# Routing nine of sixteen batches through a 103-tile expert stage, and a new instruction order in a merged attention

## What is computed

```python
x = x + tanh(g_xattn[0]) * L0_xattn(ln(x), ...)   # long convolution ("hyena")
x = x + tanh(g_ffn[0])   * L0_ffn(ln(x), gate_w, w_gate, w_up, w_down)
x = x + tanh(g_xattn[1]) * L1_xattn(...);  x = x + tanh(g_ffn[1]) * L1_ffn(...)
x = x + tanh(g_xattn[2]) * L2_xattn(...);  x = x + tanh(g_ffn[2]) * L2_ffn(...)
x = x + tanh(g_xattn[3]) * L3_xattn(...);  x = x + tanh(g_ffn[3]) * L3_ffn(...)
```

```python
probs = softmax(x @ gate_w); w, sel = top_k(probs, 8); w = w / sum(w)
pos = rank of each (token, choice) within its expert, in token order
keep = pos < 1024
y = (silu(x @ w_gate[e]) * (x @ w_up[e])) @ w_down[e]
out[token] = sum over kept choices of w * y
```

## Time and profile before

| what | value |
|---|---|
| median of 3 runs | 2677.8 us (2677.27 to 2686.52) |
| profiled execution | 2674.28 us, of which the recorded span is 2672.4 |
| PE busy | 2308.8 us, 86% of the span |
| DVE, ACT, POOL busy | 1410.1 (53%), 1123.0 (42%), 654.3 (24%) |
| hyB, where the weight loads are issued | starts at 41 us, DMA share 0.42 until 129 |
| gate0 | 143 to 190 us |
| moe | 191 to 733 us |
| l1x, l1f | 733 to 1236 us |
| l2x | 1236 to about 2103 us; one batch in its middle: 51.5 us (1600.08 to 1651.61) |
| l3x, l3f | 2103 to 2672 us; l3f from 2403, its tiles from 2513 to 2577 |

### The profile page before, as it was taken

The page is one execution under the profiler, slowest core; times in us unless marked ns, Lnnn a source line. Parts: engine busy times, 40 slices in busy tenths (PEclk is TensorE's granted clock), DMA queues, the critical chain, the costliest instruction groups (busy, mean ns, idle before and its releaser), DMA issues. The chain is left out here.

```text
span 2672.4 us, 37871 instructions
## 1 busy us (share of the span) xinstructions
PE 2308.8 (86%) x10712; PEld 1446.3 (54%) x10760; DVE 1410.1 (53%) x3456; ACT 1123.0 (42%) x3406; POOL 654.3 (24%) x894
## 2 busy tenths in 40 slices
PE   6959999999968858885899888988989477869999
PEld 3446767666645534442555555555556244436775
DVE  7951111111145547774567677667667557764233
ACT  2022222222135525553555555655555167763332
POOL 5612222222113320001333333333333100002222
PEclk9959999999989989998999999999999689989999
DMA  6100000000030000000000000000000000022342
GB/s 250 53 7 7 7 6 6 6 6 6 2 140 1 0 3 1 0 0 24 1 1 1 1 0 0 0 0 0 0 0 0 2 5 4 4 97 101 103 126 63
DMA packets 40680, 68.91 MB, mean 26 GB/s; under 512 B 6800, under 2 KB 34448, under 8 KB 39312
## 3 DMA queue, kind: packets, MB, share of 16 engines
q1 hardware_dynamic: 37520, 59.44, 6.5%
q0 software_dynamic: 3072, 8.39, 1.0%
HBM read 51.30 MB, written 16.52 MB: 25 GB/s over the span
## 5 line engine op out<-in xcount | busy, mean ns | idle before, releaser
L820 DVE TENSOR_TENSOR moe_hid<-moe_act_g,moe_pU 128x384 f32<-128x384 f32 x128 | 70.9, 554 | 443.4 <-ACT moe_act_g L792 443.4
L792 ACT ACTIVATE moe_act_g<-moe_pG 128x384 f32<-128x384 f32 x128 | 62.7, 490 | 424.5 <-PE moe_pU L747 424.5
L726 POOL TENSOR_TENSOR moe_hidw<-moe_hid,moe_data_w_all 128x384 f32<-128x384 f32 x128 | 105.7, 826 | 426.7 <-DVE moe_hid L820 419.9
L979 PE MATMUL l2x_pQ<-big,l2x_xT 128*128 128x512 f32 x320 | 161.5, 629 | 39.8 <-POOL l2x_cT L2227 32.8
L2080 ACT ACTIVATE l2x_prob<-l2x_pS,l2x_nb,l2x_rms_q 128x256 f32<-128x256 f32 x256 | 142.5, 565 | 120.0 <-DVE l2x_nb L2306 120.0
L747 PE MATMUL moe_pG<-big,moe_xT 128*128 128x384 f32 x512 | 187.5, 489 | 4.1 <-POOL moe_xT L714 4.1
L768 PE MATMUL moe_pO<-big,moe_hT 128*128 128x256 f32 x768 | 186.8, 379 | 0.0
L747 PE MATMUL moe_pU<-big,moe_xT 128*128 128x384 f32 x512 | 186.3, 486 | 0.0
L2061 ACT ACTIVATE l2x_square<-l2x_pQ 128x128 bf16<-128x128 f32 x384 | 101.4, 292 | 102.2 <-PE l2x_pQ L979 102.2
L768 PEld LDWEIGHTS moe_pO<-big,moe_hT 128*128 128x128 f32 x768 | 136.0, 190 | 13.2
L747 PEld LDWEIGHTS moe_pU<-big,moe_xT 128*128 128x128 f32 x512 | 97.6, 191 | 68.3 <-issue 0.9
(11 more groups left out here) (453 smaller groups left out, 5248.7 us busy)
## 6 DMA issues: line engine op xcount, KB each, us to landing
route_x<-l3f_zero SPq DMA_DIRECT2D x1, 4992.0 KB, 16.3
l3f_xg<-route_x SPq DMA_DIRECT2D x39, 128.0 KB, 2.2
route_y<-l3f_y SPq DMA_DIRECT2D x39, 128.0 KB, 1.7
big<-in_f_gu SPq DMA_DIRECT2D x1, 4096.0 KB, 12.5
big<-in_e_gate SPq DMA_DIRECT2D x1, 3072.0 KB, 10.4
big<-in_e_up SPq DMA_DIRECT2D x1, 3072.0 KB, 17.3
big<-in_e_down SPq DMA_DIRECT2D x1, 3072.0 KB, 24.2
moe_lanes<-in_l2f_lanes SPq DMA_DIRECT2D x16, 192.0 KB, 2.8
```

The source lines that it names most:

```text
L726: pool.tensor_tensor(hidw[c % 2][:].rearrange("p (e i) -> p e i", e=n), hid[c % 2][:].rearrange("p (e i) -> p e i", e=n), bc(w, chunk // n ...
L979: last = pe.matmul(out, lhsT=xT[:, k, :], rhs=w[:, k, cols], start=(k == 0), stop=(k == KC - 1))
```

## The change

Nine batches (0 to 8) of L0_ffn are no longer computed densely. Each of their tokens goes to the 8 tiles of its 8 experts; there are (9*128*8 + 32*127)//128 = 103 tiles. Order: batches 9 to 12 dense (32 items), 103 routed tiles, batches 13 to 15 dense (24 items). The gate stage keeps the normalised tokens of batches 0 to 8 and the turned ones of 9 to 15, takes the 8 best right from the scores as each batch comes, ranks with 25 matmuls and computes the places (`slot`). The weighting of dense items moves from POOL to DVE, since POOL now scatters (72 indirect DMAs, paced by `gu_ps`, the count of finished ups) and gathers (72). The gate and up weights are laid side by side per expert (`e_gu`), and the down weights are loaded a second time with the 96 hidden rows of an expert on partitions 0 to 95 (`e_downx`), into `small`, whose own load therefore comes after the last tile. The table is cleared by one DMA from a zero input in HBM, behind the weights in hyB, and both routed stages use it.

```diff
-                G["load"](sp, "moe")
-                G["load"](sp, "small")
+                G["load"](sp, "gate")
+                G["load"](sp, "moe")
+                G["load"](sp, "zero")
...
+            if what == "zero":
+                sp.dma_start(G["route_x"].rearrange("(j p) c -> p j c", p=P),
+                             D["c_zero"].unsqueeze(1).to_broadcast([P, L0["NT"], C])).then_inc(sems["zero"], 16)
```

The gate stage, DVE and PE:

```diff
+            def best(b):
+                dve.wait_ge(logits, b + 1)
+                ch(dve.max(top[:, b, :], logit(b)))
+                ch(dve.match_replace(replaced[:, b, :], top[:, b, :], logit(b), FLOOR))
...
+            dve.tensor_scalar(chosen[:], replaced[:], FLOOR, None, ALU.is_equal).then_inc(masks, 1)
...
+            ch(dve.tensor_tensor(prod[:], need[:].unsqueeze(1).to_broadcast([P, NE, NE]),
+                                 below[:].rearrange("p (e f) -> p e f", e=NE), ALU.mult))
+            ch(dve.tensor_reduce(offs[:], prod[:], AX.X, ALU.add))
...
+            pe.wait_ge(const_in, 48)
+            pe.wait_ge(masks, 1)
+            picked = chosen[:].rearrange("p b e -> p (b e)")
+            pe.matmul(pR[:], lhsT=lower[:], rhs=picked, start=True, stop=True)
+            for d in range(1, B):
+                pe.matmul(pR[:, d * NE:], lhsT=onesb[:], rhs=picked[:, 0:(B - d) * NE], start=False, stop=True,
+                          skip_group_check=True)
+            for b in range(SB):
+                last = pe.matmul(pC[:, 0:NE], lhsT=onesb[:], rhs=chosen[:, b, :], start=(b == 0), stop=(b == SB - 1))
```

The new expert stage `phase_l0_ffn`:

```diff
+        @block.sync
+            sp.wait_ge(scattered, 16 * TOPK * SB)
+            for j in range(XR):
+                load(j)
...
+            for j in range(NT):
+                if j + 4 + XR < NT:
+                    sp.wait_ge(turned, at["routed", j + 4] + 1)
+                    load(j + 4 + XR)
+                sp.wait_ge(out_read, outs["routed", j] + 1)
+                sp.dma_start(dy[j * P:(j + 1) * P, :], y[j % YR][:]).then_inc(y_out[j % YR], 16)
...
+            sp.wait_ge(down_done, R1)
+            sp.wait_ge(combined, 1)
+            G["load"](sp, "small")
+            for n in range(lanes_early + 3, B):
+                lanes.load(sp, n)
+        @block.gpsimd
+            for b in range(SB):
+                for k in range(TOPK):
+                    pool.wait_ge(gu_ps, 1 + 5 * (TOPK * b + k) // 12)
+                    pool.indirect_dma_start(dx, bass.IndirectOffsetOnAxis(slot_i[:, b, k:k + 1], 0), G["xn_kept"][b][:],
+                                            None).then_inc(scattered, 16)
+            for r in range(YR):
+                pool.wait_ge(y_out[r], 16 * len(range(r, NT, YR)))
+            for b in range(SB):
+                if b >= GR:
+                    pool.wait_ge(combined, b - GR + 1)
+                for k in range(TOPK):
+                    pool.indirect_dma_start(yk[b % GR][:, k, :], None, dy,
+                                            bass.IndirectOffsetOnAxis(slot_i[:, b, k:k + 1], 0)
+                                            ).then_inc(yk_in[b % GR], 16)
...
+        @block.tensor
+                    pe.wait_ge(turn_read, at["routed", i] + 1)
+                    for k in range(KC):
+                        last = pe.matmul(pG[q % 2][:, 0:2 * HID], lhsT=xgT[i % 2][:, k, :],
+                                         rhs=W["e_gu"][:, k, bass.ds(expert[i] * 2 * HID, 2 * HID)], start=(k == 0),
+                                         stop=(k == KC - 1))
...
+            for q in range(Q + 2):
+                if q < Q:
+                    up(q)
+                if R0 <= q + 2 < R1:
+                    turn_routed(q + 2 - R0)
+                if 0 < q <= Q:
+                    turn_hidden(q - 1)
+                if q >= 2:
+                    down(q - 2)
...
+        @block.vector
+            def own():
+                dve.wait_ge(const_in, 16)
+                ch(dve.tensor_tensor(passed, bc(starts[:], NE),
+                                     G["until"][0:1, :].unsqueeze(1).to_broadcast([1, NT, NE]), ALU.is_ge))
+                ch(dve.tensor_reduce(owner[:], passed, AX.X, ALU.add))
+                    dve.tensor_tensor(hid[q % 2][:], act_g[q % 2][:], pU[q % 2][:, 0:CH], ALU.mult).then_inc(gated, 1)
+                    dve.wait_ge(gated, n + 1)
+                    dve.tensor_tensor(hidw[q % 2][:].rearrange("p (e i) -> p e i", i=HID),
+                                      hid[q % 2][:].rearrange("p (e i) -> p e i", i=HID),
+                                      bc(w_all[:, i, c * EC:(c + 1) * EC], HID), ALU.mult).then_inc(ready, 1)
+            def combine(b):
+                dve.wait_ge(yk_in[b % GR], 16 * TOPK * (b // GR + 1))
+                for k in range(TOPK):
+                    ch(dve.scalar_tensor_tensor(x, yk[b % GR][:, k, :], weight[:, b, k:k + 1], x, ALU.mult, ALU.add))
```

The merged attention, the slot lists of PE, ACT and POOL:

```diff
-                if at_least(b, g, 1):
-                    turn_probs(*before(b, p, g, 1), 1)
                 if at_least(b, g, 2):
                     output(*before(b, p, g, 2))
+                if at_least(b, g, 1):
+                    turn_probs(*before(b, p, g, 1), 1)
                 if g >= 2 and not last:
                     trans(b + 1, 1 - p, g - 2)
-                if at_least(b, g, 1):
-                    values(*before(b, p, g, 1), 2 * b + (1 if g == 0 else 2))
                 f_second(b, g)
                 if g < 2:
                     trans(b, p, g + 3)
+                if at_least(b, g, 1):
+                    values(*before(b, p, g, 1), 2 * b + (1 if g == 0 else 2))
                 if g == 0:
                     value_rows(b, p, 0)
...
                 exps(b, g, 1)
-                if at_least(b, g, 1):
-                    probs(*before(b, p, g, 1), 1)
-                f_middle(b, g)
                 if g == 2:
                     evacuate(b, p, 5)
                 if g < 2:
                     squares(b, p, g + 4)
                 elif not last:
                     squares(b + 1, 1 - p, 1 if g == 2 else 3)
+                if at_least(b, g, 1):
+                    probs(*before(b, p, g, 1), 1)
+                f_middle(b, g)
                 if g >= 2 and not last:
                     evacuate(b + 1, 1 - p, g - 2)
+                if g < 2:
+                    evacuate(b, p, g + 3)
                 if at_least(b, g, 1):
                     values(*before(b, p, g, 1))
-                if g < 2:
-                    evacuate(b, p, g + 3)
...
+                if g == 0 and not last:
+                    ctx(b + 1, 1 - p)
                 f_middle(b, p, g)
                 if not last:
                     if g == 1:
-                        ctx(b + 1, 1 - p)
                         unit(b + 1, 1 - p, 0)
```

The last stage: ten early batches instead of eight, batches 8 to 15 turned in one group, the routing steps some items earlier, the table's clearing removed, scatters paced from item 10 on, gathers let off by item, and the combine of batch b at R1 + 4 + 3*b//2 instead of R1 + 4 + 2*b:

```diff
-    EARLY = B // 2
+    EARLY, PACE0 = 10, 10
...
+                    pool.wait_ge(gu_ps, PACE0 + 2 * (TOPK * b + k) // 3)
...
+                pool.wait_ge(gu_ps, min(R1 + 1 + 3 * b // 2, Q))
...
-                return R1 + 4 + 2 * b
+                return R1 + 4 + 3 * b // 2
```

More of the change, by code:

```diff
@@ new lines, in scores @@
+            def scores(b):
+                pe.wait_ge(xT_ready, b + 1)
+                if b >= 2:
+                    pe.wait_ge(steps, 2 * (b - 1))
+                for k in range(KC):
+                    last = pe.matmul(logit(b), lhsT=turned(b)[:, k, :], rhs=G["l0_gate_w"][:, k, :],
+                                     start=(k == 0), stop=(k == KC - 1))
+                last.then_inc(logits, 1)
+            pe.wait_ge(*G["loaded"]["gate"])
+            turn(0)
+            for b in range(1, B):
+                turn(b)
+                scores(b - 1)
@@ L882, in _ @@
+            last.then_inc(ranks, 1)
         @block.scalar
         def _(act):
-            front_scalar(act)
-            act.wait_ge(steps, 2)
+            for b in range(B):
+                act.wait_ge(xT_ps, b + 1)
+                if 4 <= b < SB:
+                    act.wait_ge(logits, b - 3)
+                act.activation(turned(b), pT[b % 2][:, 0:C].rearrange("p (k t) -> p k t", k=KC),
+                               ACT.Copy).then_inc(xT_ready, 1)
+            act.wait_ge(steps, 2 * B + 2)
@@ new lines, in _ @@
+            nm.statistics(dve, 0)
+            nm.statistics(dve, 1)
+            for b in range(B):
+                if b % nm.GROUP == 1 and b // nm.GROUP + 2 < B // nm.GROUP:
+                    nm.statistics(dve, b // nm.GROUP + 2)
+                if b >= SB + len(nm.ring):
+                    dve.wait_ge(xT_ps, b - len(nm.ring) + 1)
+                nm.normalise(dve, b)
+                if b >= 3:
+                    best(b - 3)
+            for b in range(B - 3, B):
+                best(b)
@@ new lines, in _ @@
+            dve.tensor_scalar(chosen[:], replaced[:], FLOOR, None, ALU.is_equal).then_inc(masks, 1)
+            for t in range(2):
+                L = pL[t][:, 0:B // 2 * NE].rearrange("p (b e) -> p b e", e=NE)
```

(8 more changed lines are left out.)

542 lines of the change are left out of this document (306 added, 236 removed).

## The result

| what | before | after |
|---|---|---|
| median, same chip | 2682.1 us (2677.3 to 2686.5, 4 runs) | 2560.1 us (2560.05 to 2561.84, 4 runs) |
| ratio | | 0.9551, 95% interval 0.9535 to 0.9567 |
| profiled execution | 2674.28 us, span 2672.4 | 2560.05 us, span 2558.0 |
| granted TensorE clock over the span | 0.949 | 0.942 |

A forecast was written before the change was run, and what follows sets the result against it. TensorE columns bound the first expert stage; merged attention left TensorE idle 90 us. Terms -157.8 (dense to routed), -8.2 (gate), +7.4 (waits), -5 (attention), +1.3 (last stage) took 2674.3 to 2512.0; plus 3, 2515 us, range 2500 to 2530.

The forecast's parts named there:

- The gate stage's tail: Gate stage after the last score: new tail shorter, experts start at 182.9 instead of 191.18, -8.2 us.
- R4: Rival: slow HBM-to-HBM clearing of the slot table holds up the gate stage's constants, total 2754 us; chance 0.02.
- The attention's mechanism: Merged attention: context-copy wait goes, new waits for quantised hidden (1.9) and row values (0.9); -5 us in the stage.
- R3: Rival: merged attention gains all 63.6 us of its named waits, less some rest, total 2465 us; chance 0.07.
- I take 1.404, since two shapes obey one column price: First expert stage: each new routed tile costs its 1664 columns, 1.404 us; 103 tiles add 144.6 us.
- R1: Rival: register load or SP's DMAs, not columns, set the tile at about 1.62 us, total 2537; chance 0.13.
- (e): Late expert stage: SP issues small weights after the first combine, lanes 13 to 15 behind them, +0.5 us.
- (c): Late dense items: batch 1's gathers come late and hold DVE, +1; gathers slowed inside combine steps, +1 us more.
- (d): End of the expert stage: the ninth batch's combine stands in front of the last finish, +1 us.
- R2: Rival: gathers, each 0.5 us longer beside DVE, set the late dense items, total 2545 us; chance 0.10.
- (a): Early expert stage: DVE's tile-owner operations at item 1 delay item 2's multiplies, +1.7 us.
- The last stage ... meet no wait: Last stage: ten early batches, pacing and removed clearing cost nothing; only combines and late gathers at the end add 1.3 us.

The follow-up runs named there:

- e8: Changed kernel with TensorE's and ScalarE's attention lists as before, only POOL's context copy one slot earlier; 2544.7 us, ratio 0.9396.
- e2: Changed kernel with tile weights sliced by constants (expert i mod 32), the register load and its check kept but unused; 2551.4 us, tiles 1.411 us.
- e3: Changed kernel without SP's 97 loads of tiles 6 to 102, stores kept; 2575.4 us, tiles 1.629 us.
- e6: Changed kernel without the bounds check on the expert's number loaded into the TensorE register; 2551.3 us, tiles 1.411 us.
- e9: Changed kernel without the first expert stage's 72 gathers and their combines, small weights issued right after the last tile; 2537.2 us.
- e12: Changed kernel with the edits of e6 and e8, and small weights issued only after seven batches are combined; 2499.8 us, ratio 0.9327.
- e14: Changed kernel with the edits of e6 and e8, and the last stage's routing steps at their old places; 2521.2 us, ratio 0.9318.
- e5: Changed kernel, unedited, run again on another chip; 2572.8 us, ratio 0.951.
- e10: Changed kernel with the whole merged attention as before, lists and context copy; 2568.1 us, ratio 0.9579.

## Why the prediction was wrong

**Right.** The gate stage's tail, -8.2 against -8.1. Dense items at 4.20. The first tile's turn, 2.2 against 2.05. The clearing, costed at nothing and put at 124: issued at 44.2 it landed 79.6 us later, at 123.8, and nobody waited (R4 falls). The last stage's tiles. The attention's mechanism: new waits of 1.7 for the hidden (1.9 forecast) and of up to 0.8 for the row values (0.9), a batch of 51.1. R3 falls for this order; with the old lists and only the copy moved (e8) the stage is 42.5 us shorter than before, where the forecast had 5 and R3 55.

**Wrong, first: "I take 1.404, since two shapes obey one column price".** The tile of the earlier trace rows sat where two limits nearly meet: 1920 columns need 1.62 us, and the same kinds of register instruction need 1.636 in the new tile. It could not tell me which binds, and I read it as proof for columns. What fails is the overlap: I let the columns hide all register work, and 1664 columns do not. R1 had the size right, 1.62 and +22, and half of the cause: load and check alone (e2) leave 1.411, SP's DMAs (e3) have no part, and it takes the slices' arithmetic on top. Measured is 1.636 over 94 tiles, 94 x (1.636 - 1.404) = +21.8, and e6 takes it away. It deserved the larger chance: the only row with the same registers showed 1.62.

**Second: (e), +0.5 for the small weights.** I priced only what SP issues late, not what 4.2 MB of weights (the 22 sizes in the DMA view sum to that, not to the 4.9 of the expectations) do to batch 1's gathers and to the lane behind them. With (c) and (d) I had 3.5 us; the waits were 1.24 + 7.14 + 2.98 + 0.23 = 11.6. e9 ties them to gathers, combines and the weights' place together; e12 puts 7.3 of 11.7 down to the weights. R2's cause, DVE steps that hold gathers back, is not it: 72 gathers took 70.2 us, 0.975 each, beside nine combines at 0.486 a step. The Trainium skill's exclusive lock ("SBUF — State Buffer", Who interferes with whom) costs little here: of the three gathers that start inside batch 0's combine (515.65, 516.89, 518.14) two took 0.94 and 0.95 us and one 1.07, and over all 72 the mean is 0.03 above 0.945, not the 0.5 of R2. (a) was 3.20 for 1.7.

**Third: "The last stage ... meet no wait".** True of tiles and clearing, not of the moved routing steps, which I put at nothing without a reason: +6.6 by e14.

**Fourth: scatter and the clock.** Two parts of the chain came out longer with no line of them changed: +4.8 in L1's stages, +6.0 in L3's attention. The rows of L3's attention show a lower clock, same stretch, before and after:

```profile
2185.00:2235.00 50.00, 41.45 (x293) 25.08 (x292) 40.05 (x100) 37.65 (x103) 3.52 (x9) 0.97 0.02 6
```

```profile
2057.00:2107.00 50.00, 41.81 (x257) 24.93 (x257) 35.14 (x88) 33.07 (x90) 2.83 (x9) 0.85 0.02 5
```

But nothing ties this to the change. The same code took 487.9 to 489.0 us in nine of the sixteen later traces of L1's stages and 492.2 to 493.5 in seven (before 488.3, after 493.0), and 291.7 to 301.3 in L3's attention (before 295.2, after 301.1). These 10.8 us lie within the scatter of single executions; why the clock differs between them was not tried.

In the experts' stretch 37.0 us were missing. Tiles are 21.8 of them and waits 8.8: 16.8 measured, less the 7.4 forecast and the 0.6 that the kernel before had in this stretch (one wait of 0.63 us). The other 6.4 are nearly all clock: the first two items took 7.6 us up to their first transposes, where before they took 6.8, and behind three of the waits the first six downs took 2.4 to 2.6 us instead of 1.3.

The attention gave 7.9 us more than forecast. Twelve full batches at 51.06 us instead of 51.53 are 5.7 of the 12.9; another 5.6 come from five batches that ran at clock 0.97 before and took 52.1 to 53.2 us. The changed kernel has none such, and neither have e5 and e8; e10, with the old lists and copy, has seven of twelve again. The sum: +21.8 + 8.8 + 6.4 + 1.2 + 4.8 - 7.9 + 6.0 + 6.8 = +47.9, from -162.3 to -114.4.

## What to carry to other kernels

- A row that satisfies two limits at once proves neither. Before an operation is made smaller, ask what else each instance of it needs (register loads, bounds checks, address arithmetic), and take the time of the like operation as its floor until an edit shows otherwise. Here dropping a bounds check on a value that was clamped already gave 21 us over 94 tiles.
- A moved load is priced by what is in flight beside it at the new place, not by its issue: here gathers landed in 6.9 us beside it and in 2.8 without. And in an in-order list, moving one late item (the context copy) gave 28 us more than moving it with the list around it.
- Before a stage's difference in one trace is explained, look how far the same code scatters in the others: 4 to 10 us here.

## What I had not expected of the hardware

- TensorE reports itself busy 99% of a stretch that its register instructions slow down by 16%; the third to the eighth tile still ran at full rate (1.41), then 1.64. Only starts tell.
- Three chips ran the kernel before about 1% slower (2707 to 2710 us against 2679 to 2682) and showed ScalarE idle for 5 to 17 us at a time beside the first expert stage's gathers and combines, with no releaser named; not beside the 72 scatters, nor when gathers and combines were left out.
- Routing steps moved to a stage's start, 64 matmuls of 8 columns bunched and waits behind them, kept the granted clock at 0.83 instead of 1.00 for 20 us, 6.6 us in all.
